# A DLRM tower with pairwise products: four stages of 256 rows in place of two of 512, larger and later sums, three groups looked up by one-hot columns

## The reference

```python
e = stack([tbl_f[ids[:, f]] for f in range(32)], axis=1)   # 1024 x 32 x 64
p, q = e[:, ROW], e[:, COL]                                # the 496 pairs
kp = einsum('bpj,ipj->bpi', p, kernel)
z = sum(kp * q, axis=-1)                                   # 1024 x 496
h = concatenate([z, dense_ctx], axis=1)                    # 1024 x 512
h = maximum(h @ W_top1 + b_top1, 0)                        # 512
h = maximum(h @ W_top2 + b_top2, 0)                        # 256
y = h @ W_top3
```

## Time and profile before

| | |
|---|---|
| median of 3 runs | 588.83 us (588.6 to 599.1) |
| the profiled execution | 586.51 us |
| its span | 584.7 us |
| PE busy | 440.4 us, 75% |
| DVE busy | 291.5 us, 50% |
| POOL busy | 242.4 us, 41% (256 gathers) |
| ACT busy | 59.9 us, 10% |
| chain of waits, by engine | PE 65%, another core or an unknown queue 15%, issue 14%, DVE 5% |

### The profile page before, as it was taken

One profiled execution on the slowest core, in us unless ns is written; L12 is line 12 of the kernel. 1 busy time (PEld: TensorE's weight loads), 2 busy tenths in 40 slices (PEclk: granted clock), 3 DMA queues, 4 the chain that ended last, 5 costly groups with the idle time before them and its releaser, 6 DMA issues.

```text
span 584.7 us, 5769 instructions
## 1 busy us (share of the span) xinstructions
PE 440.4 (75%) x2216; PEld 148.8 (25%) x2216; DVE 291.5 (50%) x250; ACT 59.9 (10%) x85; POOL 242.4 (41%) x260
## 2 busy tenths in 40 slices
PE   0105213858969998889885293799999999999998
PEld 0002001213323232223231031232323333333442
DVE  0001001536748677668661261576768788885000
ACT  0000100101010101000200110011001200020212
POOL 5777773545635551350667567166550000000000
PEclk9998655969989999899998588699999999999999
DMA  3112111112312222221311411011110000000000
GB/s 121 27 27 53 27 27 32 46 36 70 80 33 72 64 55 58 60 55 37 80 23 28 144 25 27 4 42 23 21 24 18 2 1 0 1 19 1 1 0 0
DMA packets 15404, 21.33 MB, mean 36 GB/s; under 512 B 5521, under 2 KB 5777, under 8 KB 15250
## 3 DMA queue, kind: packets, MB, share of 16 engines
q0 software_dynamic: 8192, 8.40, 7.7%
q1 hardware_dynamic: 6464, 11.80, 6.8%
q10 hardware_dynamic: 722, 0.76, 0.4%
HBM read 18.85 MB, written 0.00 MB: 32 GB/s over the span
## 4 chain that ended last, share of the span: by engine, by line
PE 65%; another core or an unknown queue 15%; issue 14%; DVE 5%; DVEq 0%; ACT 0%
PE kp L372 36%; PE z_ps L388 19%; DVE prod L344 5%; PE kp L409 5%; PE kp L414 2%; PE tr_ps L357 2%; PE kp L419 1%; DVEq L343 0%; ACT prod L312 0%; DVEq L342 0%; DVEq L340 0%
## 5 line engine op out<-in xcount | busy, mean ns | idle before, releaser
L344 DVE TENSOR_TENSOR prod<-kp,pair 128x1024 f32<-128x1024 f32 x248 | 290.1, 1219 | 242.7 <-remote 113.1
L255 POOL DMA_INDIRECT raw<-in_tbl,ids_sb x256 | 242.2, 946 | 194.2 <-PE tr_ps L357 92.2
L372 PE MATMUL kp<-pair,k_sb 64*128 64x512 f32 x992 | 253.9, 637 | 89.0 <-DVE prod L344 48.6
L372 PEld LDWEIGHTS kp<-pair,k_sb 64*128 64x128 f32 x992 | 87.7, 193 | 237.2 <-issue 134.4
L388 PE MATMUL z_ps<-prod,ones_sel 128*32 128x512 f32 x992 | 128.7, 640 | 0.0
L357 PE MATMUL tr_ps<-ident,raw 128*128 128x128 f32 x128 | 24.1, 318 | 52.9 <-DMA raw<-in_tbl,ids_sb 47.6
L270 ACT ACTIVATE pair<-tr_ps 128x512 f32<-128x512 f32 x32 | 19.1, 598 | 346.0 <-PE tr_ps L357 181.8
L388 PEld LDWEIGHTS z_ps<-prod,ones_sel 128*32 128x32 f32 x992 | 27.0, 114 | 91.4 <-issue 70.9
L357 PEld LDWEIGHTS tr_ps<-ident,raw 128*128 128x128 f32 x128 | 15.5, 157 | 77.6 <-issue 43.1
L409 PE MATMUL kp<-z_sb,w_sb 128*128 128x512 f32 x64 | 28.2, 596 | 0.0
L280 ACT ACTIVATE pair<-pair 64x1024 f32<-64x1024 f32 x16 | 16.9, 1055 | 0.4
(11 more groups left out here) (5 smaller groups left out, 1.0 us busy)
## 6 DMA issues: line engine op xcount, KB each, us to landing
k_sb<-in_kd SPq DMA_DIRECT2D x31, 256.0 KB, 2.6
raw<-in_tbl,ids_sb POOLq DMA_INDIRECT x256
pair<-pair SPq DMA_DIRECT2D x16, 128.0 KB
w_sb<-in_w SPq DMA_DIRECT2D x1, 1024.0 KB
z_sb<-in_dense ACTq DMA_DIRECT2D x2, 256.0 KB
w_sb<-in_w SPq DMA_DIRECT2D x1, 512.0 KB
ids_sb<-in_ids ACTq DMA_DIRECT2D x1, 128.0 KB, 3.4
ident<-in_ident ACTq DMA_DIRECT2D x1, 64.0 KB
```

The source lines that it names most:

```text
L255: nc.gpsimd.indirect_dma_start(raw[:, g % RAW_RING, b, n, :], None, tables[f], bass.IndirectOffsetOnAxis(ap=ids_sb[:, h, b, f:f + 1], axis=0),
L344: nc.vector.tensor_tensor(prod[:, slot % PROD_RING, :, :], kp[slot % KP_RING][:, :, :], factor, ALU.mult).then_inc(prod_done, 1)
L372: last = nc.tensor.matmul(kp[slot % KP_RING][:, q, :], k_sb[rows, s, :], pair[rows, h * GROUPS + owner // 2, :], start=True, stop=True)
```

## The change

The batch goes in four *stages* of 256 rows (`WIDTH`). A *unit* is two slots of a stage: its `kp` and `prod` have the size of a slot before (4 tiles of 256 columns in place of 2 of 512), and there are 248 units. A group of a stage is 2 blocks, a `raw` entry of 4 gathers; the ring has 16 entries. In the first stage a transposing *event* is one group, later two. All of `k_sb` is now read in each stage, and loaded in the first, 8 slots at a time. Sums go in batches of 5, 6, 5 units, 4 units behind the batch's end; `prod` is a ring of 12. The slot order puts mixed pairs later and the even owner always first.

Six fields with tables of 1,000 rows are moved into groups 0, 2 and 4. In the first stage these are not gathered: SP loads the two tables (125 partitions x 8 rows) and a group's ids on all partitions, DVE makes one-hot columns by 16 comparisons a group, and PE multiplies. The tables lie in the end of `k_sb`, the one-hot columns in `prod`. The MLP's weights are loaded over `k_sb` in the last stage, and the MLP goes layer by layer, the last layer's halves side by side. The diff, cut:

```diff
-KP_RING = 3
-PROD_RING = 2 * BATCH_SLOTS
-RAW_RING = 4
+K_LOAD = 8
+K_AHEAD = 3
+KP_RING = 3
+PROD_RING = 12
+RAW_RING = 16
+WIDTH = 256
+STAGES = (1, 2, 2, 2)
+BATCH_UNITS = (5, 6, 5)
+LOOKUP = (0, 2, 4)
+SMALL_P, SMALL_C = 125, 8
...
+TRANSPOSE_AT = [0, 0, 0, 1, 2, 4, 7, 10, 13, 17, 20, 25, 31, 36, 41, 47, 52, 57, 61, 66, 71, 77, 87, 93, 98, 109,
+                114, 119, 128, 133, 139, 149, 155, 160, 171, 176, 181, 190, 195, 201]
...
+            load_hot_ids(0)
+            sp.dma_start(row_sb[0:SMALL_P, :], row_no).then_inc(row_no_in, 16)
+            load_tables(0)
+            load_hot_ids(1)
+            load_tables(1)
+            load_k(0)
+            load_hot_ids(2)
+            load_tables(2)
+            for j in range(1, K_AHEAD):
                 load_k(j)
...
+                if st == LAST and s == W_SLOTS:
+                    sp.wait_ge(kp_done, u)
+                    sp.dma_start(w1_sb, w1).then_inc(weights_in, 16)
...
+            for r, (g, b) in enumerate(GATHER):
+                if r >= RAW_RING and EVENT_OF[r - RAW_RING] != (EVENT_OF[r - RAW_RING - 1] if r > RAW_RING else None):
+                    pool.wait_ge(transposed, EVENT_OF[r - RAW_RING] + 1)
+                for i in range(2):
+                    for n in range(2):
+                        f = 2 * g + n
                         nc.gpsimd.indirect_dma_start(
+                            raw[:, r % RAW_RING, i, n, :], None, tables[f],
...
+            dve.wait_ge(row_no_in, 16)
+            for i in range(len(LOOKUP)):
+                dve.wait_ge(hot_ids_in[i], 16)
+                for c in range(SMALL_C):
+                    for n in range(2):
+                        nc.vector.tensor_scalar(hot(i, n, c), hot_ids_sb[0:SMALL_P, i, n, :],
+                                                row_sb[0:SMALL_P, c:c + 1], None,
+                                                ALU.is_equal).then_inc(hot_ready, 1)
...
+                    pe.wait_ge(table_in[lookup], 2 * 16)
+                    for c in range(SMALL_C):
+                        for i in range(2):
+                            pe.wait_ge(hot_ready, 2 * (SMALL_C * lookup + c) + i + 1)
+                            last = nc.tensor.matmul(tr_ps[64 * i:64 * i + 64, 0:WIDTH],
+                                                    table_sb[0:SMALL_P, lookup, i, c, :], hot(lookup, i, c),
+                                                    start=(c == 0), stop=(c == SMALL_C - 1), skip_group_check=True)
...
+            def products(u):
+                st, s = UNIT[u]
+                if u >= KP_RING:
+                    pe.wait_ge(prod_done, u - KP_RING + 1)
+                for i, x in enumerate(unit_slots(u)):
+                    if st == 0 and x % K_LOAD == 0:
+                        pe.wait_ge(k_in[x // K_LOAD], 16)
+                    for q in range(2):
+                        owner = SLOT[x][q][0]
+                        rows = slice(64 * q, 64 * q + 64)
+                        pe.wait_ge(evacuated, group_event(st, owner // 2) + 1)
+                        last = nc.tensor.matmul(kp[u % KP_RING][:, q, i * WIDTH:(i + 1) * WIDTH], k_sb[rows, x, :],
+                                                pair[rows, group_place(st, owner // 2), :],
+                                                start=True, stop=True)
                 last.then_inc(kp_done, 1)
...
+            for u in range(UNITS):
+                for e in events_at(u):
+                    transpose_event(e)
+                products(u)
+                b = BATCH_OF[u]
+                if b and u == summed_behind(b - 1):
+                    reductions(b - 1)
```

More of the change, by code:

```diff
@@ L68 @@
 assert len(SLOT) == SLOTS
-assert all((a[0] + b[0]) % 2 for a, b in SLOT)
+assert all(a[0] % 2 == 0 and b[0] % 2 == 1 for a, b in SLOT)
 def partners(tile):
@@ L107, with group_place, mixed_place, factor_place @@
[L107 to L115, removed]
+def group_place(st, k):
+    return GROUP_AT + GROUPS * (st % 2) + k
+def mixed_place(i, m):
+    if i == 0:
+        return MIX0_ODD if m % 2 else MIX0_EVEN
+    return MIX1_AT + m % MIX1_RING
+def factor_place(st, tile):
+    factor, m = tile[1]
+    return group_place(st, factor) if m is None else mixed_place(factor, m)
@@ new lines, in summed_behind, with chunk_end, mix_unit, mixed_free @@
+def summed_behind(b):
+    st, first, n = BATCHES[b + 1]
+    return first + min(LAG, n) - 1
+def chunk_end(st, c):
+    t = min((c + 1) * CHUNK_TILES, TILES) - 1
+    return BATCH_OF[unit_at(st, t // 2)]
+def mix_unit(st, m):
+    k = min(2 * m + 2, GROUPS - 1)
+    return unit_at(st, next(s for s in range(SLOTS) if SLOT[s][0][1] == (k, None))) + 2
+def mixed_free(st, m):
+    places = [mixed_place(i, m) for i in range(2)]
+    before = [u for u in range(mix_unit(st, m)) for s in unit_slots(u) for tile in SLOT[s]
+              if tile[1][1] is not None and mixed_place(*tile[1]) in places]
+    return max(before) + 1 if before else 0
@@ new lines, in gather_order, with lookup_of @@
+def gather_order():
+    gathers, events = [], []
+    for st, n in enumerate(STAGES):
+        for k in range(0, GROUPS, n):
+            first = len(gathers)
+            if st or k not in LOOKUP:
+                gathers += [(g, st) for g in range(k, k + n)]
+            events.append((st, k, n, range(first, len(gathers))))
+    return gathers, events
+GATHER, EVENT = gather_order()
+EVENT_OF = [e for e, (st, k, n, raws) in enumerate(EVENT) for r in raws]
+def lookup_of(e):
+    st, k, n, raws = EVENT[e]
+    return LOOKUP.index(k) if st == 0 and k in LOOKUP else None
@@ L179, in pairwise_tower, with mixed_use @@
         y_stored = sem("y_stored")
[L182 to L183 removed]
+        MLP = [(1, h, n) for h in range(HALVES) for n in range(N1)]
+        MLP += [(2, h, n) for h in range(HALVES) for n in range(N2)] + [(3, 0, 0)]
         def mlp_at(layer, h, n):
             return MLP.index((layer, h, n))
[L188 to L205, removed]
+        def mixed_use(st, m):
+            return st * (FOURS // MIX1_RING) + m // MIX1_RING
         block = ctx.enter_context(nc.Block())
@@ L227, in _ @@
-            for j in range(3):
-                load_k(j)
[L229 to L241, removed]
+                first, end = K_LOADS[j]
@@ L362, in products @@
-            def products(slot):
-                h, s = divmod(slot, SLOTS)
-                if h == 0 and s % BATCH_SLOTS == 0:
-                    pe.wait_ge(k_in[s // BATCH_SLOTS], 16)
-                if slot >= KP_RING:
-                    pe.wait_ge(prod_done, slot - KP_RING + 1)
-                for q in range(2):
-                    owner = SLOT[s][q][0]
-                    rows = slice(64 * (owner % 2), 64 * (owner % 2) + 64)
-                    pe.wait_ge(evacuated, h * GROUPS + owner // 2 + 1)
-                    last = nc.tensor.matmul(kp[slot % KP_RING][:, q, :], k_sb[rows, s, :],
-                                            pair[rows, h * GROUPS + owner // 2, :], start=True, stop=True)
-                last.then_inc(kp_done, 1)
@@ L442 @@
     tables = [_np.asarray(inputs[f"tbl_{f}"]) for f in range(FIELDS)]
+    small = [f for f in range(FIELDS) if tables[f].shape[0] == SMALL][:2 * len(LOOKUP)]
+    others = [f for f in range(FIELDS) if f not in small]
+    field_at = [small.pop(0) if i // 2 in LOOKUP else others.pop(0) for i in range(FIELDS)]
+    tables = [tables[f] for f in field_at]
     pair_no = {}
```

433 lines of the change are left out of this document (248 added, 185 removed).

## The result

The changed kernel took 630.8 us (median of 4 runs, 626.8 to 634.6) beside 593.97 for the kernel before (588.6 to 600.6: the three runs of the table above and a fourth): 1.071 times as long, 95% interval 1.060 to 1.083. The forecast was 570 us in 490 to 615, and faster. The profiled execution took 631.76 us, its span is 629.8.

A forecast was written before the change was run, and what follows sets the result against it. Bound: 415 us of PE work, plus some 123 lost, mostly to late PE signals under gathers. Unit 24 at 134.6, units 303, transposes 21, tail 47.2 make 506; gathers' 60 makes span 566, time 570 us; range 490 to 615.

The forecast's parts named there:

- at 0.325 they cost 60: After unit 24, the 148 gathers left (185 us) lose 0.325 us per us of streaming, adding 60 us.
- 11.2 us for each signal: While gathers stream without a pause, news that PE has finished reaches the other engines 11.2 us late per signal.
- twice as many matmuls to a signal: Stated way to be wrong: late signals get worse with doubled matmuls per signal; no size given.
- Unit 24: End of the late start: PE reaches this unit at 134.6 us, some 10 us behind the first run of gathers.
- The tail: From the first MLP matmul to the span's end: 47.2 us, down from 49.3, with last-layer halves side by side.
- Up to some 50 us they come in time, as before: At the start, PE's signals are on time until some 50 us, and PE reaches unit 20.
- Rival (c): POOL hardly pauses between double groups, so 0.57 is lost per us over 185 us of gathers: 615 us; chance 0.10.
- the long first run: First stage: POOL gathers until block 24 has no room, 96 gathers ending at 124.4 us.
- rival (d): Narrow sums of 256 columns start no faster: 0.2145 us more for each of 496 rounds, 106 us, 676; chance 0.05.
- the 106 or 43 of the bounds: Extra us for narrow PE rounds: 106 if sums keep today's round, 43 at 0.058 for each of 744 added rounds.
- Rival (a): Whole kernel: PE's signals are on time for a reason not seen, giving 435 us; chance 0.13.
- 462 us for a kernel before that loses nothing: Kernel before: first slot at 46.8 us plus 415 us of PE work, of a 584.7 us span.

## Why the prediction was wrong

**The step that failed** is the forecast's "at 0.325 they cost 60": the loss per us of gathers was carried from the kernel before, where a signal stood for 8 PE instructions, to one where it stands for 16. The number that would have corrected it was in the prediction: "11.2 us for each signal" is 8 times 1.40, and the runs show 1.40 us for each instruction (22.40 for 16, 28.00 for 20). It named "twice as many matmuls to a signal" as what would make it wrong, and gave it no case of its own.

Term by term, in the forecast's own sum. Unit 24 starts at 151.0 us, forecast 134.6: **16 more.** From there 224 units at 1.40 are 314, forecast 303: **11 more.** The transposes, 21, stay as forecast. The tail is **0.5 more.** That makes 151 + 314 + 21 + 47.7 = 533, and the span is 629.8: 96 us lost from there on, while 148 gathers (185 us) run, 0.52 per us where the sum had 0.325: **36 more.** 566 + 16 + 11 + 0.5 + 36 = 630, rounded. Doubling 0.325 would give 0.65; the 20 gathers in fours cost nothing, and the 128 behind them (160 us) cost 0.6. How much of this rate is the doubling and how much the pattern of runs, no run separates in the changed kernel; in the kernel before the doubling alone multiplied the loss by 1.9.

*Start.* "Up to some 50 us they come in time, as before" failed with it. The kernel before had only a few transposes to signal there, 8 instructions a group in 10 us; the look-up has 64 in one signal, and nothing was on time from the first. The run of gathers ended at 89 us, not at 124, since no more than group 1, the first that was gathered, had been signalled. The last gather came at 441 us, not at about 390. Rival (c), the slower side, came nearest with 615, but for want of pauses; they were there, in 26 runs of gathers, and 0.52 was lost all the same.

*Ring.* The prediction had the long first run in its sum (96 gathers to 124.4 us), but never as a cost of the 16 blocks: it has no case of a shorter ring. A ring of 4 wins back 39 us, because the first run of gathers can't last till nothing more is signalled.

*Narrow rounds.* Right in the main: rival (d) is out. The narrow rounds cost 0.03 us a unit over before, and twice the instructions without lateness cost the kernel before 10 to 11 us, 2.3 to 2.5%, in place of the 106 or 43 of the bounds. The Trainium skill (TensorE: Matmul & The Clock Gate, "Back-to-back issue gap") would have had 54, by the estimate in the prediction. Its 81 ns is for matmuls of 128 columns, and these have 256; the trace goes below it all the same, with 40 loads and 40 matmuls of the sums, four side by side, in 2.30 us, 58 ns a pair.

*Look-up.* 0.31 to 0.32 us a comparison, forecast 0.33, and POOL's gathers beside them went at 1.25 us: the warning of the Trainium skill (SBUF — State Buffer, "SBUF: two separate sides") did not bear on these comparisons.

*Rival (a), on time,* gave 435; four versions took 450 to 455 in on-time sessions. 12 of the difference are 248 units at 1.40 in place of 1.353. The prediction's own 462 us for a kernel before that loses nothing was near the 472 of its spans there; that this kernel has sessions in which nothing is late, no row told.

**What stays open.** What makes a session late, and by what path gathers reach PE's signals; whether it is their length, rate or descriptors, since the runs for it met on-time sessions; and why an instruction costs 0.70 at first and 1.40 later. The granted clock is not what makes it late: two runs of the version without the look-up took 633.6 us at 0.892 and 635.7 at 0.962. A rival that no run tests is the recording itself: no run on record is known to have gone without it, and the trace holds a record for each instruction, so twice the instructions are twice the records. The Trainium skill (NOTIFIC — the notification-queue block, "Overflow: three behaviours, one of which stalls the engine") has, as one of three settings, that a full queue of such records stalls the engine that writes them. A cost by instruction would fit it; no run here shows or excludes it.

## What to carry to other kernels

When a signal of an engine comes late, divide the delay by the instructions that the engine issued for it before you carry it over: here 11.20 over 8 and 22.40 over 16 gave one number, and halving the tiles of the kernel before made its loss 1.9 times as large. A deeper ring of gathers is no free cover: it also sets how long gathers may run without a pause, so try it at both ends. And time the kernel before in each session: it took 474 and 587 us.

## What was not expected of the hardware

- In late sessions a PE instruction under a long run of gathers costs 0.70, then 1.40 us, loads and matmuls alike, while 40 loads and 40 matmuls of the products take 4.73 us once the gathers are over. Twenty gathers in fours with 2.7 to 4.3 us between cost nothing; mostly in eights, gathers cost 0.5 to 0.6 us for each us that they run, in fours with mostly 1.2 to 2.2 us between 0.40.
- PE runs ahead of what the others have heard: 32 matmuls and 32 loads were over in 6.4 us, and ACT started on their signal 37.6 us later.
- The granted clock is lower where PE idles: 0.57 from 44 to 94.6 us, and 0.858 over the span of the kernel with twice the instructions, late, against 0.986 for it on time.
